# Gradient loop turned by one tile, and three moves in the FFN rows: heads between squares, a normalisation between shifted copies, a turned tile between rotations

## What is computed

```python
h = shift_token(x)
q, k, v = split(h @ wqkv)                  # 8 heads of 64
q, k = rotary_xpos(l2norm(q) * qs, l2norm(k) * ksc)
x = x + local_attention(q, k, v) @ wo      # windows of 64, look-back one window
h = layernorm(shift_token(x)) * lg + lb
a, g = split(h @ w1 + b1)
x = x + (a * gelu(g)) @ w2 + b2
```

```python
h = swish(k @ gate) * (k @ val)            # k: (2048, 128), gate, val: (128, 512)
pred = h @ proj                            # proj: (512, 128)
loss = mean((pred - v) ** 2)
for _ in range(2):
    grads = grad(loss)
    theta = {n: theta[n] - 0.1 * newton_schulz(grads[n]) for n in theta}
```

## Time and profile before

| | us |
|---|---|
| median of 3 runs | 2460.48 |
| lowest, highest run | 2440.2, 7308.2 |
| the profiled execution | 2457.95 |
| its span | 2456.1 |

### The profile page before, as it was taken

One profiled execution on the slowest core, in us unless ns is written; L12 is line 12 of the kernel. 1 busy time (PEld: TensorE's weight loads), 2 busy tenths in 40 slices (PEclk: granted clock), 3 DMA queues, 4 the chain that ended last, 5 costly groups with the idle time before them and its releaser, 6 DMA issues.

```text
span 2456.1 us, 43351 instructions
## 1 busy us (share of the span) xinstructions
PE 1927.0 (78%) x14817; PEld 1210.1 (49%) x14880; DVE 1605.8 (65%) x2479; ACT 1240.6 (51%) x2826; POOL 1063.8 (43%) x838
## 2 busy tenths in 40 slices
PE   2799989859898896589898862995687888884596
PEld 1455555425555554355555531882344544632485
DVE  5687888357979976678887735783443444336486
ACT  2467666357979975366666642343322222234242
POOL 2555666146767765355665505232231123003333
PEclk9899999867979978699999975997898999996798
DMA  6000000020000101000000022004000000000202
GB/s 218 1 2 2 2 2 1 15 77 17 22 19 22 26 18 42 0 2 2 2 2 2 2 103 77 18 23 140 0 0 0 0 0 0 0 0 16 66 23 67
DMA packets 43928, 63.32 MB, mean 26 GB/s; under 512 B 7504, under 2 KB 33488, under 8 KB 42736
## 3 DMA queue, kind: packets, MB, share of 16 engines
q1 hardware_dynamic: 39232, 51.96, 6.9%
q0 software_dynamic: 4544, 9.35, 1.2%
HBM read 45.26 MB, written 21.18 MB: 27 GB/s over the span
## 4 chain that ended last, share of the span: by engine, by line
PE 23%; issue 17%; DVE 7%; POOL 6%; ACT 5%; DMA 2%; SPq 0%; POOLq 0%; DVEq 0%; ACTq 0%
POOL sorted_x L2018 3%; PE PS L1723 3%; PE PS L1705 2%; PE PS L448 2%; POOL arena L2411 2%; DVE arena L757 1%; PE PS L1707 1%; PE PS L1706 1%; PE PS L482 1%; ACT arena L635 1%; PE PS L1713 1%; PE PS L500 1%; DVE arena L770 1%; DMA arena<-sorted_x 1%; PE PS L266 1%
## 5 line engine op out<-in xcount | busy, mean ns | idle before, releaser
L1497 POOL TENSOR_TENSOR arena<-arena 128x1024 f32<-128x1024 f32 x128 | 299.9, 2365 | 144.0 <-ACT arena L1431 144.0
L635 ACT ACTIVATE arena<-PS,arena 128x128 f32<-128x128 f32 x512 | 180.6, 370 | 123.9 <-DVE arena L784 123.6
L949 POOL TENSOR_TENSOR arena<-arena 128x512 f32<-128x512 f32 x128 | 133.3, 1043 | 253.5 <-DVE arena L791 251.5
L1405 PE MATMUL PS<-con,arena 128*128 128x128 f32 x1024 | 163.4, 307 | 45.6 <-DVE arena L1481 44.2
L318 PE MATMUL PS<-arena_r 128*128 128x512 f32 x216 | 118.2, 547 | 90.5 <-DVE arena_r L1918 43.2
L757 DVE SCALAR_TENSOR_TENSOR arena<-PS,fcol,big 128x512 f32<-128x512 f32 x256 | 177.1, 742 | 12.7 <-PE PS L320 6.6
L1405 PEld LDWEIGHTS PS<-con,arena 128*128 128x128 f32 x1024 | 124.4, 155 | 121.2 <-issue 96.5
L1431 ACT ACTIVATE arena<-PS,arena 128x512 f32<-128x512 f32 x256 | 155.1, 688 | 56.1 <-DVE arena L1462 54.5
L1481 DVE COPY arena<-PS 128x512 f32<-128x512 f32 x256 | 166.3, 685 | 24.8 <-PE PS L1405 24.5
L1442 ACT ACTIVATE arena<-arena 128x512 f32<-128x512 f32 x256 | 162.6, 636 | 23.3 <-DVE arena L1469 17.2
L1462 DVE TENSOR_REDUCE arena<-PS 128x4 f32<-128x2048 f32 x64 | 146.7, 2292 | 29.3 <-PE PS L1387 29.3
(11 more groups left out here) (366 smaller groups left out, 4865.0 us busy)
## 6 DMA issues: line engine op xcount, KB each, us to landing
big<-in_gu SPq DMA_DIRECT2D x16, 512.0 KB, 8.3
sorted_x<-in_slots SPq DMA_DIRECT2D x2, 2515.5 KB, 14.6
arena<-sorted_x SPq DMA_DIRECT2D x6, 774.0 KB, 7.3
big<-in_dn SPq DMA_DIRECT2D x16, 256.0 KB, 8.7
arena<-expert_y SPq DMA_DIRECT2D x16, 256.0 KB, 3.3
big<-in_wqkv SPq DMA_DIRECT2D x2, 1536.0 KB, 8.6
arena<-q_split SPq DMA_DIRECT2D x96, 32.0 KB
arena<-k_split SPq DMA_DIRECT2D x96, 32.0 KB
```

The source lines that it names most:

```text
L635: act.activation(pr[:, u % 2, t, :], PS[:, u % 2, t * P:(t + 1) * P], ACT.Exp, bias=nmax[:, u % 2, t:t + 1], accum_out=psum_[:, u % 2, t:t ...
L949: g.tensor_tensor(pn[:, u % 2, :, :], pr[:, u % 2, :, :], pinv[:, u % 2, :].unsqueeze(2).broadcast_to([P, TPB, P]), ALU.mult).then_inc(s(" ...
L1405: tr = pe.transpose(PS[:, 4 + t % 2, kt * P:(kt + 1) * P], pp[:, st % 2, t, kt * P:(kt + 1) * P], ident)
L1497: g.tensor_tensor(a, a, mk[:, hp, 2 * half:2 * half + 2, :], ALU.mult).then_inc(s("a_masked"), 1)
```

## The change

Gradient. The forward part of tile 0 is taken out of the loop body: it stands once ahead of the loop, and again at the end of the body, for the next batch row. On PE it goes between the dh of tile 3 and the three gradient products of tile 3; on ACT behind the copy of the turned dp; on DVE behind the last du and dg and ahead of the three additions; on POOL only the staging of the keys moves. The last batch row is written out once behind a loop of three, without a next tile 0. Values get four banks (2, 3, 6, 7) in place of two. Products of tiles 2 and 3 wait no more for `g_w` but for the silu of tile t-2 (`g_silu`), and tile 2 for the previous row's additions (`grad_added`), because banks 6 and 7 also hold gradients. ACT and POOL still wait for `g_w`.

FFN. ACT: `take_heads(r, 3)` goes between the two squares of pair 3. DVE: `take_turned(r, 4)` goes between the two halves of `rotate` for pair 0. POOL: `normalised(r, 1)` goes ahead of `shifted(r, 1)` in place of behind it.

```diff
@@ ffn_act row
                 norm(1)
-                square(3)
+                if nx is not None:
+                    squares(nx, 3, (1,))
                 take_heads(r, 3)
+                if nx is not None:
+                    squares(nx, 3, (0,))
                 norm(2)
@@ ffn_dve row
-                rotated(0)
+                if nx is not None:
+                    rotate(nx, 0, (0,))
                 take_turned(r, 4)
+                if nx is not None:
+                    rotate(nx, 0, (1,))
                 maxima(r, 6)
@@ ffn_pool shifted, rows
-                if i == 2:
+                if i == 1:
                     g.wait_ge(s("p_normed"), START + at(N, UNITS, 2))
...
                 shifted(r, 0)
+                g.wait_ge(s("v_shifted"), START + V + 2)
+                normalised(r, 1)
                 shifted(r, 1)
-                g.wait_ge(s("v_shifted"), START + V + 4)
-                normalised(r, 1)
                 shifted(r, 2)
@@ gradient loop
+        VAL_BANK = (2, 3, 6, 7)
+        def over_rows(eng, one):
+            with eng.Fori(0, B - 1) as b:
+                one(b, False)
+            one(B - 1, True)
...
+            def gate_value(n, t):
+                kt = k_s[:, t * P:(t + 1) * P]
+                pe.matmul(PS[:, t % 2, :], kt, th_g[:], start=True, stop=True).then_inc(s("g_gate"), 1)
+                pe.matmul(PS[:, VAL_BANK[t], :], kt, th_v[:], start=True, stop=True).then_inc(s("g_val"), 1)
...
                 for t in range(TPB):
-                    kt = k_s[:, t * P:(t + 1) * P]
-                    pe.wait_ge(s("g_w"), START + at(n, TPB, max(t - 1, 0)))
-                    if t < 2:
+                    if t == 1:
                         pe.wait_ge(s("g_dg"), START + at(n, TPB))
-                    pe.matmul(PS[:, t % 2, :], kt, th_g[:], start=True, stop=True).then_inc(s("g_gate"), 1)
-                    pe.matmul(PS[:, 2 + t % 2, :], kt, th_v[:], start=True, stop=True).then_inc(s("g_val"), 1)
+                    if t == 2:
+                        pe.wait_ge(s("grad_added"), START + at(n, 3))
+                    if t >= 2:
+                        pe.wait_ge(s("g_silu"), START + at(n, TPB, t - 1))
+                    if t:
+                        gate_value(n, t)
...
                     if t < TPB - 1:
                         dh(t + 1)
+                    elif not last:
+                        pe.wait_ge(s("staged"), START + at(n, 2, 3))
+                        pe.wait_ge(s("g_dg"), START + at(n, TPB, TPB - 1))
+                        gate_value(n + 1, 0)
...
+            def sigmoids(n, t):
+                act.wait_ge(s("g_gate"), START + at(n, TPB, t + 1))
+                act.wait_ge(s("g_w"), START + at(n, TPB, max(t - 1, 0)))
...
+            sigmoids(B * step, 0)
...
                 act.activation(dp_tok.rearrange("p a b -> p (a b)"), PS[:, 4, :], ACT.Copy).then_inc(s("dp_tok_ready"), 1)
+                if not last:
+                    sigmoids(n + 1, 0)
...
+                if not last:
+                    v.wait_ge(s("g_used"), START + at(n, TPB, 1))
+                    v.wait_ge(s("g_dg"), START + at(n, TPB, TPB))
+                    gated(n + 1, 0)
                 v.wait_ge(s("grads"), START + at(n, 2, 2))
...
+                if not last:
+                    stage_keys(n + 1, b + 1)
```

More of the change, by code:

```diff
@@ L601, in entered, with squares @@
                 act.activation(h_hi[64:128, WINDOW + 1:WINDOW + L], y[64:128, b, 0:L - 1], ACT.Copy).then_inc(s("h_ready"), 1)
-            def squares(r, j):
+            def squares(r, j, halves=(1, 0)):
                 N = of_row(f, r)[0]
                 act.wait_ge(s("sq_summed"), START + reuse(N, PAIRS, j, 2))
-                for half in (1, 0):
+                for half in halves:
                     if half:
@@ L751, in rotate @@
                 v.wait_ge(s("qk_rotated"), START + 2 * reuse(N, PAIRS, j, 2))
-                for half in range(2):
+                for half in halves:
                     v.wait_ge(s("proj"), START + at(N, 2 * PAIRS, 2 * j + half + 1))
@@ L2342, in grad_pe, with one @@
                     pe.matmul(PS[:, 7, :], kt_s[:, t, :], dg[:, t % 2, :], start=st, stop=sp_).then_inc(s("g_used"), 1)
+            over_rows(pe, one)
         def grad_act(act, step):
-            with act.Fori(0, B) as b:
+            def sigmoids(n, t):
+                act.wait_ge(s("g_gate"), START + at(n, TPB, t + 1))
+                act.wait_ge(s("g_w"), START + at(n, TPB, max(t - 1, 0)))
+                act.activation(sg[:, t % 2, :], PS[:, t % 2, :], ACT.Sigmoid).then_inc(s("g_sig"), 1)
+                act.activation(g_m[:, t % 2, :], PS[:, t % 2, :], ACT.Sigmoid, scale=-1.0).then_inc(s("g_sig"), 1)
+            sigmoids(B * step, 0)
+            def one(b, last):
                 n = b + B * step
-                for t in range(TPB + 1):
+                for t in range(1, TPB + 1):
                     if t < TPB:
-                        act.wait_ge(s("g_gate"), START + at(n, TPB, t + 1))
-                        act.wait_ge(s("g_w"), START + at(n, TPB, max(t - 1, 0)))
-                        act.activation(sg[:, t % 2, :], PS[:, t % 2, :], ACT.Sigmoid).then_inc(s("g_sig"), 1)
-                        act.activation(g_m[:, t % 2, :], PS[:, t % 2, :], ACT.Sigmoid, scale=-1.0).then_inc(s("g_sig"), 1)
-                    if t >= 1:
-                        act.wait_ge(s("h_turned"), START + at(n, TPB, t))
-                        if t == 1:
-                            act.wait_ge(s("predicted"), START + n)
-                        act.activation(hT[:, :, (t - 1) * P:t * P], PS[:, 4, :].rearrange("p (a b) -> p a b", a=4),
-                                       ACT.Copy).then_inc(s("hT_ready"), 1)
+                        sigmoids(n, t)
+                    act.wait_ge(s("h_turned"), START + at(n, TPB, t))
+                    if t == 1:
+                        act.wait_ge(s("predicted"), START + n)
+                    act.activation(hT[:, :, (t - 1) * P:t * P], PS[:, 4, :].rearrange("p (a b) -> p a b", a=4),
+                                   ACT.Copy).then_inc(s("hT_ready"), 1)
                 act.wait_ge(s("dp_turned"), START + n + 1)
@@ L2370, in grad_dve, with gated, one @@
             v.wait_ge(s("grad_zero"), START + step + 1)
[L2371 removed]
+            def gated(n, t):
+                v.wait_ge(s("g_sig"), START + at(n, 2 * TPB, 2 * t + 2))
+                v.tensor_tensor(th_s[:, t, :], PS[:, t % 2, :], sg[:, t % 2, :], ALU.mult).then_inc(s("g_silu"), 1)
+                v.wait_ge(s("g_silu"), START + at(n, TPB, t + 1))
+                v.wait_ge(s("g_val"), START + at(n, TPB, t + 1))
+                v.tensor_tensor(th_h[:, t, :], th_s[:, t, :], PS[:, VAL_BANK[t], :], ALU.mult).then_inc(s("g_h"), 1)
+            v.wait_ge(s("g_used"), START + at(B * step, TPB))
+            gated(B * step, 0)
+            def one(b, last):
                 n = b + B * step
[L2373 removed]
+                for t in range(1, TPB + 1):
                     if t < TPB:
[L2375 to L2376 removed]
+                        if t == 1:
                             v.wait_ge(s("g_used"), START + at(n, TPB))
[L2378 to L2384 removed]
+                        gated(n, t)
+                    v.wait_ge(s("g_slope"), START + at(n, 2 * TPB, 2 * t))
+                    v.tensor_tensor(th_w[:, t - 1, :], g_d[:, (t - 1) % 2, :], PS[:, VAL_BANK[t - 1], :], ALU.mult).then_inc(s("g_w"), 1)
                 v.wait_ge(s("predicted"), START + n + 1)
@@ L2397, in grad_dve, with stage_keys @@
                     v.tensor_tensor(grad[:, i, :], grad[:, i, :], PS[:, bank, :], ALU.add).then_inc(s("grad_added"), 1)
+            over_rows(v, one)
         def grad_pool(g, step):
-            with g.Fori(0, B) as b:
-                n = b + B * step
-                g.wait_ge(s("k_tok_ready"), START + B)
+            def stage_keys(n, b):
                 g.wait_ge(s("g_val"), START + at(n, TPB))
@@ L2405, in grad_pool, with one @@
                 g.tensor_copy(k_s, kT[:, b, :]).then_inc(s("staged"), 1)
+            g.wait_ge(s("k_tok_ready"), START + B)
+            stage_keys(B * step, 0)
+            def one(b, last):
+                n = b + B * step
                 for t in range(TPB):
```

23 lines of the change are left out of this document (8 added, 15 removed).

## The result

| | before | after |
|---|---|---|
| median of the timed runs | 2453.66 us | 2373.65 us (2364.44 to 2379.05) |
| ratio to before | 1 | 0.9707, interval 0.967 to 0.9744 |
| profiled execution | 2457.95 us, span 2456.1 | 2364.44 us, span 2362.6 |

One of the four timed runs of the kernel before took 7308.2 us; the ratio is formed from the other three (2440.2, 2446.85 and 2460.48) and those of the kernel after, so it is not the quotient of the two medians above.

A forecast was written before the change was run, and what follows sets the result against it. PE, busy 78%, was taken as the bound, with gains only where it waits. Gradient 42 us (31 + 7 + 4) plus FFN 5 made 47 us off the profiled 2457.95: 2411 us, range 2392 to 2436.

The forecast's parts named there:

- FFN, heads between the squares: FFN, ACT: heads copied some 1.3 us earlier, PE loses its 1.28 wait, but DVE's gapless run covers it: nothing gained.
- Gradient, the turn: Gradient loop: dp comes 5.2 us earlier in each of six turns, 31 us.
- Gradient, the entry: First batch row of each step: silu 0 to dp shortens from 16.2 to 12.7 us, twice, 7 us.
- Gradient, the clock: Gradient loop: shorter PE waits win back 4 of the 5 us lost at the lower clock level.
- No table load in the loop: Gradient loop: expected sign, two table loads for the sigmoid in place of eight.
- the case without cover: FFN: if DVE's run did not hide it, PE's 1.28 in 14 rows would give 18 us.
- Rival 2: Gradient loop: a table load at the head of the body, 1.3 us in six turns, 2419 us; chance 0.12.
- FFN, the normalisation: FFN, POOL: layer norm scale L301 falls to about 1.05 us, 0.45 in 14 rows, less in four: 5 us.
- Rival 3: FFN: POOL's copies come late for `values`, some 0.7 in 14 rows lost and 5 not won, 2426 us; chance 0.13.
- FFN, the turned tile: FFN, DVE: same six operations in another order, nothing gained; bounds 3 us won and 10 lost.
- Rival 1: FFN: PE's path really sets the row, so the heads give 18 us in place of 5, 2398 us; chance 0.15.
- Rival 4: Gradient loop: denser work is granted the lower clock, whole loop there some 2520 us; chance 0.03.

The follow-up runs named there:

- the heads alone: Kernel before with only the ACT edit, the copy of the heads put between the two squares of pair 3: 2424.09 us, ratio 0.9925.
- four copies on ACT: Kernel after with four small ACT copies of 28 columns put ahead of the norm of pair 2: 2395.72 us, ratio 0.9778.
- the pause on DVE: Kernel after with a one-column DVE copy put ahead of the first of the four scales: 2384.85 us, ratio 0.9747.
- The long hold: Kernel before with POOL's sum of pair 3 held back until all four scales are written: 2451.76 us, ratio 1.0029.

## Why the prediction was right or wrong

In short: the gradient part came out as argued. What failed is the term "FFN, heads between the squares", put at nothing because DVE's run of four scales covers it; it is worth some 18 us. Another 13 us of the distance between 2411 and 2373.65 is the starting point, an execution that much above the usual time of the kernel before, and some 7 us is the gradient part (49 timed, 42 forecast).

**Gradient, the turn: right.** 5.2 us a turn were forecast, 5.1 measured between undisturbed turns. The sum over absolute distances hit gate 2 and dp within 0.15 us. It had no step that parted banks and turn, and needed none.

**Gradient, the entry: one term left out.** 3.5 each was forecast, 4.5 and 4.3 measured. The sum counted the way from the silu of tile 0 to dp: that was 16.2 us and is 13.4 and 13.0, so it gives 2.9 and 3.2. The other 1.7 and 1.1 lie ahead of this silu, where the prediction put nothing. ACT in step two, before and after:
```profile
1952.64 1.28 ACT L2351 ACT_TABLE_LOAD   x1 [4.58 <-PE PS L2308]
...
1879.59 1.28 ACT L2378 ACT_TABLE_LOAD   x1
1884.36 0.60 ACT L2378 ACTIVATE arena<-PS 128x512 f32<-128x512 f32 x1 [3.49 <-PE PS L2296]
```
Before, the load waited for the first gate product (started at 1951.04) and the sigmoid for the load. Now it is done at 1880.87, ahead of the gate product (1882.25). In step two the first gate product itself took longer, 2.08 us against 1.51.

**Gradient, the clock: right in size, as far as one pair of profiles tells.** The loop windows give 34.2, six turns of 5.1 make 30.6, which leaves 3.6 (forecast 4): the granted mean rose from 0.94 and 0.96 to 0.98. In the other profiles of the old loop there was 3.4 more to win in step two. One turn in each step (31.4) still lies 1.3 to 1.6 above the others.

**No table load in the loop: right.** In the groups of the kernel after:
```profile
L2378 ACT ACT_TABLE_LOAD x2 | 2.6, 1283 | 0.0
```
Two loads in place of eight. Rival 2 is refuted. The Trainium skill (ScalarE: Activation LUTs, section What ACT_TABLE_LOAD costs) gives a load of some 1283 ns and a drain of some 1380 ns for a switch of set. The trace shows the first number and not the second: the load of the earlier trace rows starts 0.10 after the gate product is done (1986.70 + 1.02), ends at 1989.10, and the sigmoid starts at 1989.11.

**FFN, heads between the squares: wrong, and here the prediction failed.** The step reads "I cost it at nothing: the cover is DVE's gapless run until 1232.17". The run was gapless only as a merged row shows it. It took a length of 4.62 as a property of the four scales, when it was the result of a collision, whose trigger was the norm that this very edit moves. The page had the hint: a mean of 1169 ns for a shape whose single instructions take 0.6 when nothing meets them, and 4.62 / 4 is 1.16. The step asked what an earlier copy of the heads does, and not what else stands behind it in ACT's queue. The cover fell together with the wait it covered. Measured: 18 us by the timed runs (10 to 27), 16 over the rows of both stages in the profile of the heads alone, in place of 0. The value given for the case without cover, 18, came out, but by luck: it was 1.28 us in 14 rows, PE's wait alone, where it is 1.57 at most 12 times, because the scales shrank with it.

**FFN, the normalisation: right in kind, small.** 0.45 a row was taken as half way, 0.6 measured. L301 takes 0.77, for the normalisation (L955, 274.18 to 275.22) is nearly done when it starts, at 274.99. The next copy is recorded from 275.37 on, while L301 runs, and it is the copy that is stretched:
```profile
275.37 0.86 POOL L970 COPY arena<-arena 64x512 f32<-64x512 f32 x1 [0.16 <-POOL arena L955]
```
So the fear that a copy would lengthen L301 to 1.05 or 1.36 did not come true; the two met the other way round. Rival 3 is refuted, narrowly: the last copy ends at 279.39 and PE starts `values` at 279.44. The 1.6 us of room are gone, and in 10 of the 14 rows PE stands idle there for 0.02 to 0.03 us, where it did not before. An edit that shortens the row further may make the copies late.

**FFN, the turned tile: right**, nothing (1.0014).

**Rival 1** named the right edit, the right sign and, at 2398, a closer number than the forecast. Its reason, that PE's path alone sets the row, is refuted by the run with four copies on ACT, where PE does not wait for the heads and the row is still 1.4 us longer, and by the pause on DVE. The long hold agrees with it as far as it goes: with the heads late, short scales give nothing. **Rival 4** is refuted: the clock rose. Its figure of 2520 us for the whole loop at the lower level is too low by its own terms: 28 us of products in each of eight batch rows, doubled, add 224 to 2411.

**Sum.** 42 became 43.0 in the profiles (49 by the timed runs), 5 became 21.7 (21). The lower end of the range has a slip: rival 1 with 18 for the heads and the full 11 at L301 is 2457.95 - 42 - 18 - 11 = 2387, not 2392, since the 5 that was taken off had already been replaced. 2373.65 lies under both. From 2445 us, the usual time of the kernel before, that sum would have given 2374, near the measured time; that is luck, for rival 1's reason is refuted. The forecast itself had no case in which the cover shrinks.

The Trainium skill (SBUF — State Buffer, section Who interferes with whom) has the two engines exclude one another for whole instructions, by order of issue. The runs agree on the exclusion: 0.6 became 1.7 us, about 0.6 and POOL's 1.2. The recorded start did not tell who goes first. With POOL already waiting, DVE mostly went on through successors that followed without a pause (74 of 84 rows), and let POOL in at a pause of 0.04 us (before) or 0.07 us (four copies on ACT). The page's rule was weighed for L301 only; the scales are the same kind of operation.

## What to carry to other kernels

Where a cost is set to nothing because another engine's run covers it, open that run into single instructions and compare each with the shortest of its shape; a stretched one is a collision, and what the change moves may be its trigger. Two paths of nearly equal length need the table of four cases, since each fix alone can show nothing or next to it (0.0 and 0.2 us a row here). An absolute time sheet of a loop, made from measured distances, held here to 0.15 us. And start a forecast from the usual time of the kernel, not from the one execution that was profiled: here they lay 13 us apart, a quarter of the forecast gain, and unchanged code differed by 17 us between two profiles.

## What was not expected of the hardware

- Four DVE operations of 128x512 with two SBUF inputs take 2.48 us without a pause, and 4.62 with one pause of 0.04 us (before) or 0.07 us (four copies on ACT) in front of the third while POOL waits, the last two at some 1.7 each. With a pause ahead of the first they take 4.62 too. In 10 of 84 rows without a recorded pause they took 4.62 all the same, with the second one stretched.
- POOL's recorded duration holds the time it stood blocked: 1.26, 2.43 and 3.62 us for the same sum, with some 1.2 of its own work in each. So a longer POOL row can be the sign of a faster DVE.
- Which of the two is recorded as starting first, by 0.01 to 0.03 us, decided nothing in these rows.
- The new gradient loop, entered with its table set in place, does no load in its passes. The old one loaded in each of its eight passes, 1283 ns each, with nothing behind it.
